# A feed-forward and attention kernel: pieces of the weights' preparation stand in another order on VectorE and ScalarE between the first rounds

## The reference, cut to what matters

```python
x = x + 0.5 * ffn(layernorm(x))
x = x + attention(layernorm(x))        # linear attention, 16 heads
x = x + 0.5 * ffn(layernorm(x))

def ffn(x):                            # q = fp4 in blocks of 16, with one scale per block
    gate, up = q(x) @ q(w_gate).T, q(x) @ q(w_up).T      # 256 -> 704
    return q(silu(gate) * up) @ q(w_down).T              # 704 -> 256
```

## Time and profile before

| what | value |
|---|---|
| median of 3 runs | 2159.74 us (2159.51 to 2160.04) |
| the profiled execution, its own time | 2161.74 us |
| its span, first to last instruction | 2159.9 us |
| mean granted TensorE clock | 0.995 of full speed |
| PE busy | 2095.1 us, 97% of the span |
| DVE busy | 2042.0 us, 95% |
| ACT and POOL busy | 89% each |
| DMA engines, hardware queue | 47.1% |

### The profile page before, as it was taken

How to read it: one execution, slowest core, us unless ns; L and a number is a source line. 1 busy time by engine, 2 the same in 40 slices (tenths; PEclk the granted TensorE clock), 3 DMA queues, 4 the chain that set the end, 5 groups by cost and what they waited for, 6 DMA issues and landing times.

```text
span 2159.9 us, 88415 instructions
## 1 busy us (share of the span) xinstructions
PE 2095.1 (97%) x30384; PEld 1509.9 (70%) x30384; DVE 2042.0 (95%) x5231; ACT 1922.4 (89%) x4137; POOL 1915.0 (89%) x3002
## 2 busy tenths in 40 slices
PE   3899999999999999999999999989999999999998
PEld 1566666666666689999999999975666666666665
DVE  7999999999999889999999999989999999999997
ACT  7888888888888799999999999998888888888885
POOL 5899999999999878888888888889999999999996
PEclk9999999999999999999999999999999999999999
DMA  4665555555556432222233222325555555555555
GB/s 104 131 122 115 116 115 115 116 115 115 114 114 115 85 63 62 62 62 62 62 63 62 62 62 62 63 51 90 117 115 115 115 115 115 115 115 114 115 116 117
DMA packets 719840, 208.49 MB, mean 97 GB/s; under 512 B 666400, under 2 KB 719520, under 8 KB 719776
## 3 DMA queue, kind: packets, MB, share of 16 engines
q1 hardware_dynamic: 719776, 207.76, 47.1%
HBM read 20.38 MB, written 16.78 MB: 17 GB/s over the span
## 4 chain that ended last, share of the span: by engine, by line
PE 92%; DVE 4%; issue 2%; ACT 1%; DMA 1%; POOL 1%; SPq 0%; POOLq 0%; DVEq 0%; ACTq 0%
PE ffn_ps_gu L960 40%; PE ffn_ps_down L972 21%; PE attn_ps_qk L1402 8%; PE attn_ps_sc L1449 5%; PE attn_ps_num L1435 4%; PE attn_ps_v_second L1415 4%; PE attn_ps_z L1479 4%; PE attn_ps_num L1440 2%; PE attn_ps_kT_first L1410 1%; PE attn_ps_z L1476 1%; PE attn_ps_kT_first L1467 1%; DVE ffn_per_block L785 1%; DVE ffn_hx L774 0%; DVE ffn_y L823 0%; DMA x_sb<-in_L_ffn_w_up 0%
## 5 line engine op out<-in xcount | busy, mean ns | idle before, releaser
L960 PE MATMUL ffn_ps_gu<-wgu_hi,ffn_xT 128*128 128x512 f16 (+1 forms) x3072 | 739.7, 364 | 13.4 <-DVE ffn_hx L774 6.2
L960 PEld LDWEIGHTS ffn_ps_gu<-wgu_hi,ffn_xT 128*128 128x128 f16 x3072 | 301.3, 98 | 300.2 <-issue 19.3
L960 PE MATMUL ffn_ps_gu<-wgu_lo,ffn_xT 128*128 128x512 f16 (+1 forms) x1536 | 432.0, 363 | 0.0
L867 POOL TENSOR_TENSOR ffn_h_hl<-ffn_q,ffn_h_scale_hi 128x704 f16<-128x704 f16 x256 | 352.4, 1376 | 28.5 <-DVE ffn_q L815 9.2
L888 ACT ACTIVATE ffn_quarter<-ffn_y,offsets 128x960 int16<-128x960 f32 (+2 forms) x264 | 282.4, 1070 | 99.0 <-DVE ffn_y L823 97.0
L972 PE MATMUL ffn_ps_down<-wd_hi,ffn_hT 128*128 128x256 f16 x2816 | 349.3, 273 | 8.9 <-DVE x_sb L799 5.9
L868 POOL TENSOR_TENSOR ffn_h_hl<-ffn_q,ffn_h_scale_lo 128x704 f16<-128x704 f16 x256 | 355.2, 1388 | 0.0
L972 PEld LDWEIGHTS ffn_ps_down<-wd_hi,ffn_hT 128*128 128x128 f16 x2816 | 274.5, 98 | 69.8 <-issue 7.9
L785 DVE TENSOR_REDUCE ffn_per_block<-ffn_hx 128x60 f32<-128x960 f32 (+2 forms) x264 | 298.0, 1129 | 5.4
L823 DVE TENSOR_TENSOR ffn_y<-ffn_hx,ffn_per_block 128x960 f32<-128x960 f32 (+2 forms) x264 | 292.6, 1108 | 0.0
L878 ACT ACTIVATE ffn_silu<-ffn_ps_gu,unscale 128x704 f32<-128x704 f32 x256 | 215.4, 841 | 76.9 <-PE ffn_ps_gu L960 74.9
(11 more groups left out here) (186 smaller groups left out, 5254.3 us busy)
## 6 DMA issues: line engine op xcount, KB each, us to landing
x_sb<-in_L_attn_x SPq DMA_DIRECT2D x128, 128.0 KB, 2.4
out<-x_sb SPq DMA_DIRECT2D x128, 128.0 KB, 2.1
attn_v_eo<-attn_v_nat SPq DMA_DIRECT2D x256, 34.0 KB, 1.8
ffn_xT<-ffn_x_hl SPq DMA_TRANSPOSE x256, 2.5
ffn_hT<-ffn_h_hl SPq DMA_TRANSPOSE x256, 3.5
attn_xT<-attn_x_hl SPq DMA_TRANSPOSE x128, 2.4
attn_oT<-attn_o_hl SPq DMA_TRANSPOSE x128, 2.5
x_sb<-in_L_ffn_w_gate SPq DMA_DIRECT2D x2, 352.0 KB, 4.6
```

What stands on the lines that cost most here:

```text
L867: nc.gpsimd.tensor_tensor(blocks(h_hl[par][:, 0:INNER]), blocks(q[par][:, 0:INNER]), over_block(h_scale_hi[par][:], HB), ALU.mult)
L960: last = nc.tensor.matmul(ps_gu[par][:, a:b], xT[par][:, c, :], w[:, k, a:b], start=(n == 0), stop=(n == len(terms) - 1))
```

## The change: five pieces move on VectorE, two on ScalarE

Instructions are neither added nor removed. What moves, seen from one list at a time:

- DVE: `lower(1)` stands ahead of `lower(0)`; the four copies `copies_lo` stand behind round -2 and no longer ahead of it; `tops(1)` stands ahead of round -1 and no longer behind it; `values(2)` stands ahead of the attention's powers and no longer behind them.
- ACT: `masks` stands behind round -2 and no longer at the very start; `upper(2)` (down) stands ahead of the attention's `upper`.
- PE, POOL and SP keep their lists.

```diff
@@ vector
             in_order(dve, ffn_step, -3, -2)
+            of_ffn.lower(dve, 1)
             of_ffn.lower(dve, 0)
-            of_ffn.lower(dve, 1)
+            in_order(dve, ffn_step, -2, -1)
             of_ffn.copies_lo(dve)
-            in_order(dve, ffn_step, -2, -1)
             of_attn.tops(dve)
+            of_ffn.tops(dve, 1)
             in_order(dve, ffn_step, -1, 0)
-            of_ffn.tops(dve, 1)
             of_ffn.powers(dve, 2, 3)
+            of_ffn.values(dve, 2)
             of_attn.take_powers(dve)
             of_attn.powers(dve)
-            of_ffn.values(dve, 2)
             in_order(dve, ffn_step, 0, 1)
             of_ffn.lower(dve, 2)
@@ scalar
             ffn_step = of_ffn_0.scalar
-            of_attn.masks(act)
             in_order(act, ffn_step, -6, -4)
...
-            in_order(act, ffn_step, -2, 0)
+            in_order(act, ffn_step, -2, -1)
+            of_attn.masks(act)
+            in_order(act, ffn_step, -1, 0)
             of_ffn.rounds(act, 2)
             in_order(act, ffn_step, 0, 1)
+            of_ffn.upper(act, 2)
             of_attn.upper(act)
-            of_ffn.upper(act, 2)
```

## The result

The changed kernel takes 2164.63 us (median of 22 runs, 2162.61 to 2167.79), the kernel before 2160.69 us (median of 22, 2157.51 to 2163.74). The ratio is 1.0018, with an interval of [1.0012, 1.0024]: slower by 3.9 us, which the interval tells from no change, and yet just inside the 0.2% (4.3 us) that the prediction counted as none. The forecast was 2160.8, +1.1 us, with 2163.6 as the upper end, so the direction held and the size did not. Of the 3.8 us between 2160.8 and 2164.63, 0.95 lie in the kernel before: the forecast started from the median of 3 runs, 2159.74. The change itself was missed by 2.8 us (3.9 in place of 1.1); even from 2160.69 the upper end of the range would lie 0.1 us too low. The profiled execution has a span of 2164.9 us, 5.0 more than before. It took 2166.78 us, 2.2 above the median of its runs; the profiled execution before lies 1.05 above the median of 22.

What follows compares the result with a forecast made beforehand. PE runs without a gap from about 112 us, so the change is worth its shift of that run's start: -2.2 + 1.8 + 1.5 = +1.1 us, giving a median of 2160.8, range 2157.4 to 2163.6.

Steps and rivals of the forecast that it cites:

- no wait for the upper half, with the later start in it: DVE's lower half of down no longer waits for ACT; round 1 starts at 54.3 in place of 56.51, -2.2 us.
- L1642 across rounds 1 and 2: POOL's L1642 holds DVE's L788 and L815; most of the gain is given back, +1.8 us.
- Item 1: Copies behind round -2: L815 held by POOL until 33.72, copies end at 35.9, PE's round 0 starts +2.5 us.
- Item 2: tops(1) ahead of round -1: DVE idles about 2 us for PE's turned maxima; round -1 starts at 42.3, +2.6.
- Item 3: Start of round 0 on DVE: 48.1, +1.5 us; the order of values and powers costs nothing.
- Item 4: Halves of down: L543 beats POOL's L851 by 0.05 us and holds it; DVE's round 1 at 54.3, -2.2 us.
- Item 5: Rounds 1 and 2 on DVE: POOL's L1642 holds L788 and L815; round 2 at 60.75, leaving -0.4 us.
- Items 6 and 7: SP's queue delays tile 4's `xT`; PE's round 4 is late, slow; DVE's starts +1.1 us, which stays to the end.
- L851 first: Rival: POOL's L851 wins the tie with DVE's L543; -0.2 to -1.1 us, 2159.1, chance 0.21.
- the slack that swallows all: Rival: PE's clock stays up in round 4, so DVE is not late; -0.4 to +0.3 us, 2159.7, chance 0.18.
- the gain of 4 us: Rival: L815 of round -2 not held, so DVE reaches round 1 4.3 us early; 2155.4, chance 0.05.
- The slower one: Rival: after round 4 five more bias pieces on DVE are held by POOL; +4.4 us, 2164.1, chance 0.06.

Runs made afterwards that it cites:

- e11: The changed kernel once more, unaltered, for a second profiled execution; ratio to the kernel before 1.0015 [1.0006, 1.0024].
- e1: The changed kernel with the four copies ahead of round -2 on DVE again; ratio to the kernel before 1.0006 [0.9997, 1.0015].
- e2: The kernel before with only the four copies moved behind round -2 on DVE; ratio 1.0008 [0.9999, 1.0017].
- e9: The kernel before with copies behind round -2 and down's values(2) and upper(2) ahead of the attention's; tops(1), swap and masks as before; ratio 1.0008 [0.9999, 1.0017].
- e7: The changed kernel with the attention's lower half on POOL one round later, behind round 2; ratio to the kernel before 1.0020 [1.0011, 1.0029].
- e3: The kernel before with only values(2) ahead of the attention's powers on DVE and upper(2) ahead of its upper on ACT; ratio 1.0010 [1.0001, 1.0019].
- e5: The changed kernel with lower(0) ahead of lower(1) on DVE again; ratio to the kernel before 1.0012 [1.0003, 1.0021].
- e6: The changed kernel with 26 unread matmuls of 256 columns added behind PE's round 3; ratio to the kernel before 1.0014 [1.0005, 1.0023].
- e10: The kernel before with SP's four transposes of the down weight's upper half ahead of its round 1; ratio 1.0004 [0.9995, 1.0013].
- e4: The changed kernel with SP's four transposes of the down weight's upper half ahead of its round 1; ratio to the kernel before 1.0002 [0.9993, 1.0011].
- e8: The changed kernel with copies ahead of round -2 again and SP's four upper-half transposes ahead of round 1; ratio to the kernel before 0.9994 [0.9985, 1.0002].
- e12: The kernel before with values(2) and upper(2) ahead of the attention's and SP's four upper-half transposes ahead of round 1; ratio 0.9995 [0.9986, 1.0004].

## Why the prediction was right or wrong

**The step that failed, in the terms of the sum.** Against before, DVE started rounds 1, 2 and 4 at -0.25, +2.2 and +5.0 us (e11: -1.25, +1.2 and +3.5). So all three terms were mis-sized, and all in one direction:

| term of the sum | said | after | e11 |
|---|---|---|---|
| no wait for the upper half, with the later start in it | -2.2 | -0.25 | -1.25 |
| L1642 across rounds 1 and 2 | +1.8 | +2.4 | +2.4 |
| PE's late, slow round 4 beyond its slack | +1.5 | +2.8 | +2.3 |
| sum | +1.1 | +5.0 | +3.5 |

The first term was the furthest off in both. Most of that is DVE's late round 0, 1.7 and 0.7 us (items 2 and 3). The third is the one that set the time at last, since DVE waits for PE in round 4. The rest of this section goes through the items in order. The prediction's own sign of being wrong, PE's run after 112 us displaced by more than 3 us, came up in both executions.

**Item 1, right.** L816 held until POOL's `centre` ended, copies from 34.39, PE's round 0 at 36.40 and 36.14 (35.9 was said); e1 and e2 show it from both sides.

**Item 2, right in kind, too small.** DVE waits for the turned maxima, but 3.25 and 2.52 us in place of 2. I priced PE's round 0 at the 5.1 us of one row. Eight executions here have it start at 36.1 to 36.6, and it took 4.8 to 6.2. Round -1 came at 43.77 for 42.3.

**Item 3.** Round 0 at 49.80 and 48.80 for 48.1: item 2's error with 0.2 us of its own. Before, round -1 lay between PE and DVE as a cover of 1.4 us, and the change takes this cover away just where item 1 makes PE late. e9 (no move of tops(1), 47.03) and e1 (no late copies, 46.95) each lack one of the two, and lose 0.5 and 0.4 us by round 0.

**Item 4, right in kind.** The tie went as predicted, by 0.05 us, and in the same way in every kernel here that has the down weight first: L851 (L852) took 2.03 or 2.04 us each time. Round 1 itself came at 56.26 for 54.3, late mostly by what round 0 was (1.7 us). The Trainium skill, "SBUF — State Buffer", section "SBUF: two separate sides", has the whole pair of ports locked by whoever starts first; by that rule DVE keeps it for its 1.62 us, and the trace agrees (54.14 to 55.76, L852 until 56.23). What was missed on top is small: round 1 waits 0.51 us for ACT.

**Item 5, right in kind.** The instruction held was L779 (2.67 us), not L788 and L815. Rounds 1 and 2 are 7.02 us apart where 6.45 was said. In e7, where L1643 stands a round later, the hold came a round later.

**Items 6 and 7, the wait of round 4.** The mechanism is the predicted one: `xT` for tile 4 behind the six transposes, PE late and slow in round 4, DVE waiting for it. The term "+1.5 (PE's late, slow round 4 beyond its slack)" was too small: DVE's wait is 2.71 and 2.27 us. To +1.5, with the -0.4 of DVE ahead of it, I had come with `xT` for tile 4 at 65.0 and a round 4 of 5.4 us up to its end. What was measured: `xT` for tile 3 1.4 us later than said (items 2, 3); a transpose that took 2.29 us for 1.28, 1.0; a load and a hand-over, 0.4; a slow round 4 longer by 0.9. Together they are 3.7 of the 3.9 us by which DVE's round 4 was missed (76.87 for 73.0; in e11 2.4 us, 75.41). Each price was the one row at hand, and each came out low; where two engines wait for each other in turn, they added up. Whether that is a fault of the method or of this case, one forecast doesn't show.

**The slack.** PE's 3.2 us ahead of DVE in round 4 was rightly read, and e2 shows it at work: PE's round 4 is 0.4 us late, and DVE waits for nobody. In the kernel before this lead was not kept: by round 11 four waits for DVE's addition had used it. The shift in round 4 and that in round 11 are the same within 0.2 us in e1, e3, e5, e6, e7, e9, e10 and e11; e2, with one hold fewer between them than before, gains 1.0, and e4, e8 and e12, with one more, lose 0.9 to 1.0, as does the changed kernel's first execution with L779 at 83.16.

**The rivals.** L851 first, and the slack that swallows all, fell. So did the gain of 4 us: L816 was held. The slower one named the bias pieces; they were held in three rounds at most (before, two), which moves round 11 by 1 us, not by 3.3. That its 2164.1 lies nearest to the measured 2164.63 is luck.

**What stays open.** The time behind round 11 differs too. With SP's transposes first (e4, e8, e10, e12) the span is 1.0 to 3.4 us shorter than round 11 says; e11's is 2.5 shorter, and the others lie within 0.8. So the premise that nothing behind 112 us takes back or adds to a loss does not hold to better than 3 us. In every kernel here PE is busy for all of 120 to 720 us, and at 1500 us the shift is that of the whole span already (e11 +1.0, e8 -2.1); the difference arises between, where PE has idle time only around the two changes of layer (720 to 790 and 1420 to 1500 us). One execution is profiled for each kernel, and the runs of one kernel cover 3 to 8 us, so whether this is the order's doing or scatter isn't settled. The masks' place was not tried alone; in the trace they run on ACT from 32.17 us, ahead of a wait of 1.81 us for DVE's `y`, so no cost of theirs is seen. The changed kernel without down-first was not tried either.

## What to carry to other kernels

When work that covers a wait is moved away, ask first whether another part of the same change makes the awaited engine later: here either part alone cost at most 0.5 us by the next round, and both together 1.8 to 3.3 in six executions. Price an engine's slow stretch by a range and not by the one row beside the place: the same block of 18 matmuls took 4.8 to 6.4 us here. Look for the transfer that stands behind others in a serial queue: where e4 put them in another order, 3.5 of the 3.9 us were gone in the runs, though a second timing and the trace leave room for less. A hold between two engines moved with the instruction that caused it: in e7 it came a round later, and 0.5 us were saved.

## What the runs showed of the hardware

- The same 18 matmuls of PE's round 0 took from 4.82 us (e7) to 6.43 us (e12), and 6.23 and 5.49 in two executions of one program. Always the first four took 1.86 or 1.87 us; what differs is how long this pace lasts.
- After 2.22 us of idle time round 4 ran at full pace, after 1.54 us too (e6); after 3.51, 4.37 and 6.11 us it began at half pace and took 6.0 to 6.3 us. The length of the idle time alone does not tell it: e11's round 3 began at full pace (1.04 us for four) after 4.07 us and e7's round 4 nearly so (1.13) after 4.45, both falling to half pace within the round, while e5's round 3 began at half pace (1.89) after 2.56 us.
- A POOL instruction on one number per row, L863, took 1.75 us beside DVE's L527 (46.91 to 48.54) and 0.27 us where it was free.
- One of the six transposes of the down weight often takes longer than the usual 1.2 to 1.3 us: the first took 2.29, 2.11, 2.13 and 2.16 us (after, e11, e6, e7), the second 1.95 in e3, the first of the lower half 1.95, 2.25 and 2.31 in e4, e8 and e12. The cause is open.
